# A fused transformer block on one core: row and context preparation one slot earlier, one low product of P at the slot's end, the first feed-forward rows in halves

## The reference, cut to what matters

```python
# x: (16, 256, 256) float32, cond_emb: (16, 256, 192); 16 heads of 64
def _attention(xq, xkv, wq, wk, wv, wo, bo):
    q, k, v = xq @ wq, xkv @ wk, xkv @ wv          # to 16 heads of 64
    attn = softmax(einsum('bihd,bjhd->bhij', q, k) * 64 ** -0.5)
    return einsum('bhij,bjhd->bihd', attn, v).reshape(B, S, 1024) @ wo + bo

h = _layernorm(x, ln1_g, ln1_b)
x = _attention(h, h, sa_wq, sa_wk, sa_wv, sa_wo, sa_bo) + x
h = _layernorm(x, ln2_g, ln2_b)
x = _attention(h, cond_emb, ca_wq, ca_wk, ca_wv, ca_wo, ca_bo) + x
h = _layernorm(x, ln3_g, ln3_b)
a, gate = split(h @ ff_w1 + ff_b1)                 # 256 -> 2 x 1024
return (a * gelu(gate)) @ ff_w2 + ff_b2 + x
```

## Time and profile before

| what | value |
|---|---|
| median of 3 runs | 1779.31 us (1778.8 to 1780.69) |
| profiled execution | 1778.15 us, span 1776.3 us |
| PE busy | 1736.4 us, 98% of the span |
| DVE busy | 1446.9 us, 81% |
| ACT busy | 1188.0 us, 67% |
| POOL busy | 1050.4 us, 59% |
| granted PE clock, mean | 0.999 |

### The profile page before, as it was taken

One profiled execution on the slowest core, in us unless ns is written; L12 is line 12 of the kernel. 1 busy time (PEld: TensorE's weight loads), 2 busy tenths in 40 slices (PEclk: granted clock), 3 DMA queues, 4 the chain that ended last, 5 costly groups with the idle time before them and its releaser, 6 DMA issues.

```text
span 1776.3 us, 43086 instructions
## 1 busy us (share of the span) xinstructions
PE 1736.4 (98%) x13824; PEld 1688.8 (95%) x13824; DVE 1446.9 (81%) x3137; ACT 1188.0 (67%) x3262; POOL 1050.4 (59%) x1791
## 2 busy tenths in 40 slices
PE   6999999999999999999999999999999998999998
PEld 5999999999999999999999999999999997888887
DVE  6888888888888888888888888888888887666664
ACT  5777777777777777777777777777777775221221
POOL 4777666666666666687777776666666654100110
PEclk9999999999999999999999999999999999999999
DMA  7766666666555555566676776666665561001000
GB/s 205 185 163 168 163 163 167 156 156 156 137 141 142 140 139 146 144 159 168 174 175 170 175 173 158 162 161 150 149 154 147 144 149 47 24 25 41 20 13 25
DMA packets 226496, 241.31 MB, mean 136 GB/s; under 512 B 68448, under 2 KB 190688, under 8 KB 226272
## 3 DMA queue, kind: packets, MB, share of 16 engines
q1 hardware_dynamic: 226272, 238.55, 54.0%
HBM read 58.08 MB, written 12.58 MB: 40 GB/s over the span
## 4 chain that ended last, share of the span: by engine, by line
PE 90%; POOL 5%; issue 3%; DVE 1%; ACT 0%; DMA 0%; SPq 0%; POOLq 0%; DVEq 0%; ACTq 0%
PE QKB L294 18%; PE PVB L354 13%; PE PTB L340 12%; PE WOP L327 9%; PE VB L313 9%; PE S L261 6%; PE S L262 6%; PE S L745 5%; PE PTB L745 5%; PE VB L758 3%; PE QKB L758 3%; PE VB L236 1%; POOL ON L647 1%; POOL VR L630 1%; POOL OT L652 1%
## 5 line engine op out<-in xcount | busy, mean ns | idle before, releaser
L410 ACT ACTIVATE PT<-S,NM 128x256 f32<-128x256 f32 x1024 | 471.7, 473 | 160.9 <-DVE NM L469 160.1
L469 DVE TENSOR_REDUCE NM<-S 128x2 f32<-128x512 f32 x512 | 329.6, 685 | 171.7 <-PE S L262 169.3
L647 POOL TENSOR_TENSOR ON<-ON,RB 128x256 f32<-128x256 f32 x256 | 188.6, 737 | 359.7 <-DVE ON L486 355.8
L429 ACT ACTIVATE PH<-PTB 128x1024 fp32r<-128x1024 f32 x256 | 263.2, 1028 | 126.0 <-PE PTB L340 125.8
L478 DVE TENSOR_TENSOR PL<-PTB,PH 128x512 fp32r<-128x512 f32 x512 | 327.3, 681 | 1.4 <-ACT PH L429 1.3
L340 PE MATMUL PTB<-IDN,PT 128*128 128x128 f32 x2048 | 265.9, 273 | 3.1 <-DVE PL L478 3.1
L261 PE MATMUL S<-RX 128*128 128x256 f32 x1024 | 256.9, 283 | 2.0 <-ACT PT L410 2.0
L262 PE MATMUL S<-RX 128*128 128x256 f32 x1024 | 256.7, 283 | 0.0
L340 PEld LDWEIGHTS PTB<-IDN,PT 128*128 128x128 f32 x2048 | 229.5, 140 | 4.5 <-ACT PT L410 3.8
L327 PE MATMUL WOP<-WO,OT 128*128 128x256 f32 x1536 | 226.5, 283 | 1.5 <-POOL OT L652 1.5
L294 PE MATMUL QKB<-HT,WA 128*128 128x256 f32 x1536 | 210.6, 287 | 6.6 <-POOL HT L552 3.6
(11 more groups left out here) (118 smaller groups left out, 3135.1 us busy)
## 6 DMA issues: line engine op xcount, KB each, us to landing
RX<-QKS SPq DMA_DIRECT2D x512, 192.0 KB, 2.9
RX<-QKS SPq DMA_DIRECT2D x512, 128.0 KB, 2.8
RB<-denominators SPq DMA_DIRECT2D x512, 64.0 KB, 2.6
out_dram<-XR SPq DMA_DIRECT2D x32, 256.0 KB, 3.0
XR<-in_x_dram SPq DMA_DIRECT2D x16, 256.0 KB, 3.1
denominators<-RDT SPq DMA_DIRECT2D x256, 16.0 KB
XR<-out_dram SPq DMA_DIRECT2D x16, 256.0 KB, 3.0
XN<-in_ctx_dram SPq DMA_DIRECT2D x16, 192.0 KB, 2.8
```

The costliest lines, as they stand in the source:

```text
L410: last = e.activation(PT[:, c % 2, j * S:(j + 1) * S], S1[:, i, qt * S:(qt + 1) * S], ACT.Exp, bias=NM[:, j:j + 1], accum_out=DEN[:, c % 2 ...
L429: e.activation(PH[:, s % 2, :], PTB[:, :, :].rearrange("p i n -> p (i n)"), ACT.Copy) \
L469: e.tensor_reduce(NM[:, i * TT:(i + 1) * TT], S1[:, i, :].rearrange("p (t s) -> p t s", t=TT), AX.X, ALU.max, negate=True).then_inc(a.dve_ ...
```

## The change

Four things are moved, and no arithmetic is added:

1. Preparation for the next sequence one slot earlier on every engine: statistics in slot 7 of the sequence before (was 0), aggregation and 1/sqrt in slot 0 (was 1), normalisation in slot 1 (was 2), context transposes in slots 0 and 1 (were 1 and 2), row transposes in slots 2 and 3 (were 3 and 4). SP loads the context in slot 5 (was 6).
2. On DVE the low product of head 0 of slot c-1 is done at the end of slot c, ahead of whatever closes the slot. The one of head 1 stays at the start of the next slot.
3. POOL splits staged weights in slots 4 to 7 (were 2 to 5; SP stages them in slot 1, was 0) and adds the bias to one tile in slot 5 and one in slot 6 (was two in slot 5).
4. The first feed-forward rows go in halves: statistics of two tiles each in ATT-9 and ATT-8, aggregation in ATT-7, normalisation of two tiles each in ATT-6 and ATT-5, four transposes each in ATT-3 and ATT-2, both through bank QKB, evacuated into the tile STG; the split by DVE at the end of ATT-1 (was ATT), as copy and subtraction of one half and then of the other.

```diff
 def pe_slot(e, sl):                       # TensorE, and the same shift in act_slot and pool_slot
-                if pair in (1, 2) and n >= B or pair in (3, 4):
+                if pair in (0, 1) and n >= B or pair in (2, 3):
                     sl.wait(e, a.dve_vf, c + 1)
-                if pair in (1, 2) and n >= B:
-                    pe_ctx(e, sl, n, pair - 1)
-                if pair in (3, 4):
-                    pe_h(e, sl, n, pair - 3)
+                if pair in (0, 1) and n >= B:
+                    pe_ctx(e, sl, n, pair)
+                if pair in (2, 3):
+                    pe_h(e, sl, n, pair - 2)
...
 def act_slot(e, sl):
-            if c == ATT - 1:
-                act_ffn_h(e, zero_ffn, 0)
+            if ATT - 3 <= c < ATT - 1:
+                act_ffn_h(e, zero_ffn, 0, c - ATT + 3)
...
+        def dve_p_low(e, s, i):
+
+            cols = slice(i * TT * S, (i + 1) * TT * S)
+            e.tensor_tensor(PL[:, cols], PTB[:, i, :], PH[:, s % 2, cols].bitcast(F32),
+                            ALU.subtract).then_inc(a.dve_pl, 1)
+
 def dve_slot(e, sl):
             if sl.has(c - 2):
-                s = c - 2
-                sl.wait(e, a.act_ph, s + 1)
-                sl.wait(e, a.pe_pv, s)
-                for i in range(2):
-                    cols = slice(i * TT * S, (i + 1) * TT * S)
-                    e.tensor_tensor(PL[:, cols], PTB[:, i, :], PH[:, s % 2, cols].bitcast(F32),
-                                    ALU.subtract).then_inc(a.dve_pl, 1)
+                dve_p_low(e, c - 2, 1)
...
+            if sl.has(c - 1):
+                sl.wait(e, a.act_ph, c)
+                sl.wait(e, a.pe_pv, c - 1)
+                dve_p_low(e, c - 1, 0)
+
             if pair == 3 and c > PAIRS:
...
+            if pair == PAIRS - 1 and c >= -1 and sl.has(PAIRS * (seq + 2)):
+                dve_await_x(e, sl, seq + 2)
+                dve_stats(e, sl, a, seq + 2)
             if prepares:
                 if pair == 0:
-                    dve_await_x(e, sl, seq + 1)
-                    dve_stats(e, sl, a, seq + 1)
+                    dve_aggregate(e, sl, a, seq + 1)
                 if pair == 1:
-                    dve_aggregate(e, sl, a, seq + 1)
-                if pair == 2:
                     if seq + 1 >= B:
                         e.wait_ge(a.pe_c, 2 * (seq + 2 - B))
                     dve_normalize(e, sl, a, seq + 1)
...
 def pool_weights(e, c):
-            if 2 <= pair < 2 + QTR and 1 <= seq <= NCH:
-                pool_split_w(e, WB, seq - 1, 2 + seq, pair - 2, 0)
+            if pair >= QTR and 1 <= seq <= NCH:
+                pool_split_w(e, WB, seq - 1, 2 + seq, pair - QTR, 0)
...
 def pool_slot(e, sl):
-            if prepares and pair == 5:
-                if seq + 1 == B:
+            if prepares and pair in (5, 6):
+                if seq + 1 == B and pair == 5:
                     e.wait_ge(d_bo, 32)
-                pool_add_bias(e, sl, a, seq + 1)
+                pool_add_bias(e, sl, a, seq + 1, pair - 5)
...
-            if prepares and pair == 1:
+            if prepares and pair == 0:
                 pool_rstd(e, sl, a, seq + 1)
...
+        def rows(chunk):
+
+            return (STG[:, 0:CW], STG[:, CW:2 * CW]) if chunk == 0 else halves(chunk)
+
         def transposes(chunk):
 
-            return (QKB, VB) if chunk == 0 else (PVB, WOP)
+            return (QKB, QKB) if chunk == 0 else (PVB, WOP)
...
 def pe_attention_slot(e, sl):
             pe_scores(e, sl)
-            if sl.c == ATT - 1:
+            if ATT - 3 <= sl.c < ATT - 1:
                 e.wait_ge(a.dve_lo, ATT)
-                e.wait_ge(a.dve_vf, ATT)
-                pe_ffn_h(e, zero_ffn, 0)
+                pe_ffn_h(e, zero_ffn, 0, sl.c - ATT + 3)
             pe_slot(e, sl)
...
 def dve_attention_slot(e, sl):
+            if c == ATT - 9:
+                e.wait_ge(a.dve_xo, B + HOLD + 2)
+                dve_stats(e, zero_ffn, fs, 0, 0, 1)
+            if c == ATT - 8:
+                dve_stats(e, zero_ffn, fs, 0, 2, 3)
             if c == ATT - 7:
-                e.wait_ge(a.dve_xo, B + HOLD + 2)
-                dve_stats(e, zero_ffn, fs, 0)
+                dve_aggregate(e, zero_ffn, fs, 0)
             if c == ATT - 6:
-                dve_aggregate(e, zero_ffn, fs, 0)
-            if c == ATT - 5:
                 e.wait_ge(a.pe_c, 2 * B)
                 e.wait_ge(a.pe_h, 4 * B)
                 e.wait_ge(a.pl_ht, 4 * B)
-                dve_normalize(e, zero_ffn, fs, 0, halves(0))
-            if c == ATT:
+                dve_normalize(e, zero_ffn, fs, 0, halves(0), (0, 1))
+            if c == ATT - 5:
+                dve_normalize(e, zero_ffn, fs, 0, halves(0), (2, 3))
+            if c == ATT - 1:
                 dve_ffn_split(e, zero_ffn, 0)
```

More of the change, by code:

```diff
@@ L302, in pe_slot @@
                 sl.wait(e, a.dve_vf, v)
-                if prepares and pair in (1, 2) and seq + 1 >= B:
-                    sl.wait(e, a.act_cf, 2 * (seq + 1 - B) + pair)
-                if prepares and pair in (3, 4):
-                    sl.wait(e, a.act_hf, 2 * (seq + 1) + pair - 2)
+                if prepares and pair in (0, 1) and seq + 1 >= B:
+                    sl.wait(e, a.act_cf, 2 * (seq + 1 - B) + pair + 1)
+                if prepares and pair in (2, 3):
+                    sl.wait(e, a.act_hf, 2 * (seq + 1) + pair - 1)
                 if v == 0:
@@ L397, in act_slot @@
             if c >= 0 and sl.has(PAIRS * (seq + 1)):
[L398 to L401 removed]
+                if pair in (0, 1) and seq + 1 >= B:
+                    act_ctx(e, sl, seq + 1, pair)
+                if pair in (2, 3):
+                    act_gain_bias(e, sl, seq + 1, pair - 2)
             if sl.has(c):
@@ L430, in act_slot, with dve_stats @@
                     .then_inc(a.act_ph, 1)
-        def dve_stats(e, sl, a, n):
-            for t in range(TT * sl.per):
+        def dve_stats(e, sl, a, n, *tiles):
+            for t in tiles or range(TT * sl.per):
                 last = e.bn_stats(ST6[:, t, :], XR[:, sl.x_cols(n, t * D, D)])
-            last.then_inc(a.dve_st, 1)
+                if t == TT * sl.per - 1:
+                    last.then_inc(a.dve_st, 1)
         def dve_aggregate(e, sl, a, n):
@@ L442, in dve_aggregate, with dve_normalize @@
             last.then_inc(a.dve_mv, 1)
-        def dve_normalize(e, sl, a, n, dest=(XN,)):
+        def dve_normalize(e, sl, a, n, dest=(XN,), tiles=()):
             sl.wait(e, a.pl_rs, n + 1)
-            for t in range(TT * sl.per):
+            for t in tiles or range(TT * sl.per):
                 last = e.tensor_scalar(dest[t // TT][:, t % TT * D:(t % TT + 1) * D], XR[:, sl.x_cols(n, t * D, D)],
                                        MV[:, t, 0:1], RSTD[:, t:t + 1], ALU.subtract, ALU.mult)
-            last.then_inc(a.dve_xn, 1)
+                if t == TT * sl.per - 1:
+                    last.then_inc(a.dve_xn, 1)
         def dve_await_x(e, sl, n):
@@ L533, in pool_rstd, with pool_add_bias @@
             e.tensor_tensor(RSTD[:, 0:tiles], VE[:, 0:tiles], MHALF[:, 0:tiles], ALU.pow).then_inc(a.pl_rs, 1)
-        def pool_add_bias(e, sl, a, n):
+        def pool_add_bias(e, sl, a, n, *tiles):
             sl.wait(e, a.dve_xn, n + 1)
-            for t in range(TT * sl.per):
+            for t in tiles or range(TT * sl.per):
                 xt = XR[:, sl.x_cols(n, t * D, D)]
                 last = e.tensor_tensor(xt, xt, BOUT[:, :], ALU.add)
-            last.then_inc(a.pl_xb, 1)
+                if t == TT * sl.per - 1:
+                    last.then_inc(a.pl_xb, 1)
         def pool_split_h(e, sl, n, k):
@@ L716, in w2, with pe_ffn_h @@
             return WA[:, 4 + f // 4, part, (f % 4) * D:(f % 4 + 1) * D]
-        def pe_ffn_h(e, sl, chunk):
+        def pe_ffn_h(e, sl, chunk, *ks):
             sl.wait(e, fs.dve_xn, chunk + 1)
-            sl.wait(e, fs.act_hf, PAIRS * chunk)
-            for k in range(KD):
+            for k in ks or range(KD):
+                sl.wait(e, fs.act_hf, KD * chunk + (k if ks else 0))
                 for t in range(2 * TT):
@@ L767, in pe_ffn, with act_ffn_h @@
                 pe_ffn_h(e, sl, chunk + 1)
-        def act_ffn_h(e, sl, chunk):
-            sl.wait(e, fs.pe_ht, PAIRS * (chunk + 1))
-            for k in range(KD):
-                last = e.activation(halves(chunk)[k], transposes(chunk)[k][:, :], ACT.Identity,
-                                    bias=LNG[:, 2, 1, k:k + 1], scale=LNG[:, 2, 0, k:k + 1])
-            last.then_inc(fs.act_hf, PAIRS)
+        def act_ffn_h(e, sl, chunk, *ks):
+            for k in ks or range(KD):
+                sl.wait(e, fs.pe_ht, KD * chunk + k + 1 if ks else KD * (chunk + 1))
+                e.activation(rows(chunk)[k], transposes(chunk)[k][:, :], ACT.Identity,
+                             bias=LNG[:, 2, 1, k:k + 1], scale=LNG[:, 2, 0, k:k + 1]).then_inc(fs.act_hf, 1)
         def act_ffn(e, sl):
@@ L1040, in weights @@
```

(6 more changed lines are left out.)

46 lines of the change are left out of this document (20 added, 26 removed).

## The result

The changed kernel takes 1789.01 us (median of 5 runs, 1787.53 to 1791.39), the kernel before 1779.31 us (median of 5 runs beside it, 1776.54 to 1781.19). The ratio is 1.0058 with a 95% interval of 1.0043 to 1.0072: slower by 9.7 us. The forecast was 1784, with a range of 1774 to 1793; 1789 is inside it, and 1 us above the 1781 to 1788 that the forecast claimed for itself.

The account below looks back on a forecast made before the run. PE, busy 98% of the span, was taken as the bound, its idle time mostly before the row transposes. Terms +17.1, -7.0, -1.0 and -3.5 sum to +5.6 us, giving 1784 us; 8-in-10 range 1774 to 1793.

Parts of the forecast that it names:

- The wait of the row transposes: PE's row transposes, slot 2: XN behind the moved product makes them wait 1.05 us in 30 places; term +17.1 us.
- The extra wait of the first sequence: Slot 2 of the first sequence: row transposes wait 1.9 us for PH, the product and XN; included in the +17.1.
- ON's loop: Plain cross-attention slots: one P-low product leaves the loop through ON to P·V, 0.11 us less in 64 slots, -7.0 us.
- the 0.11 is no wait: Rival, cross attention: the distance from P transposes to P·V belongs to the matmuls, nothing gained, 1791 us; chance 0.12.
- GpSimd: Weight splits and bias addition moved to other slots: two of PE's three waits for OT go, -1.0 us.
- The end: Last attention slots and first feed-forward rows: shorter loop, split normalisation, earlier split into RX, together -3.5 us, bounds -1 and -5.
- XN runs free of GpSimd: Rival: GpSimd's subtractions miss XN's start everywhere, transposes wait 0.81 us, growth +9.9, 1777.7 us; chance 0.26.
- XN is held twice: Rival: XN is held by subtraction, then cast or next subtraction; 1.38 us in 30 places, 1795 us; chance 0.12.
- The wait does not grow: Rival: the moved product costs XN nothing, the 16.3 us of waits stay, 1768 us; chance 0.08.

Follow-up runs that it names:

- e1: The changed kernel with VectorE's normalisation XN in slot 1 issued ahead of the moved P-low product instead of behind it: 1753.5 us.
- e3: The changed kernel with both P-low products back at the slot's start, leaving the shift, GpSimd's part and the new end: 1780.1 us.
- e4: The changed kernel with GpSimd's split of V in slot 2 waiting until XN is written: 1778.0 us.
- e2: The kernel before with only the first head's P-low product moved to the slot's end; preparation and program end untouched: 1797.3 us.
- e5: The kernel of e1 with the end of the program put back as in the kernel before: 1756.9 us.

## Why the prediction was right

*The wait of the row transposes* (+17.1, bounds +9.9 and +27.0). Mechanism and place were right: XN starts at +0.92 (+0.94 forecast), the transposes stand at +2.08 (+2.05), the slot of self attention waits 1.13 (1.09). e1, e3 and e4 show the cause from three sides. The size was low. The forecast took 1.05 for every wait; the fifteen of self attention sum to 17.1 (1.4 more than that), the fifteen of cross attention to 19.0 (3.2 more). By the slots a wait of cross attention is 1.28 in the mean, nine times 1.54 and six times 0.89. By the waits the term is 37.8 - 16.3 = +21.5. In cross attention the mechanism was only half right. The forecast let the subtraction for OT cover XN's start; it does overlap it, but in e4_pool_waits it does so as well and XN takes 0.73. What holds XN is V's CAST and the subtraction behind it. The long kind lies outside the bound of 1.38, which came from a pair of 1.30; the pair reaches 1.45.

One reading of the earlier trace rows was wrong. The prediction has XN's second instruction run beside GpSimd's CAST with no delay, and counts that against a full block. The instruction by itself, from the kernel before:

```profile
224.37 0.48 DVE L447 TENSOR_SCALAR XN<-XR,MV,RSTD 128x256 f32<-128x256 f32 x1
```

It takes 0.08 more than an undisturbed one (0.40) and ends at 224.85, 0.15 behind the CAST (224.70), as the first ends 0.15 behind the subtraction. XN was held twice there already; a CAST costs little because it is short.

*The extra wait of the first sequence* (1.9). The transposes stand at +2.78 there after a wait of 1.75, and the sequence as a whole costs the same 46.3 as before. The wait lies in the place of one of 1.60 that stood a slot later; both are inside the 37.8 and the 16.3.

*ON's loop* (-7.0). Right: 5.42 for 5.54 in four slots of each cross sequence, 60 x 0.12 = 7.2. e2 has it without the shift and e3 loses it without the move, so it is the product in the loop and nothing else. The rival "the 0.11 is no wait" falls.

*GpSimd* (-1.0). The two waits for OT went: slot 6 of sequences 1 and 2 fell from 6.27 to 5.66, 1.22 us together. That XN is held in these sequences now, since the splits have left, was not foreseen; it is inside the first term.

*The end* (-3.5). 2.30 + 1.04 = 3.3 by the stretches. Of this 1.1 comes with the move of P low alone (e2_p_low_alone against before) and 2.3 with the new end (e1 against e5). Slot ATT-4, with the wait of the earlier trace rows, fell from 7.21 to 6.31, the 0.9 of the forecast. ATT-3 takes 4.93, as forecast, but ATT-2 takes 5.22, and in ATT-1 and behind it P low of the second head stands behind other work, as PE's rows of the kernel after show.

```profile
1496.23 0.66 PE L340 MATMUL PTB<-IDN,PT 128*128 128x128 f32 x4 [0.68 <-DVE PL L465]
1499.08 0.98 PE L327 MATMUL WOP<-WO,OT 128*128 128x256 f32 x6 [0.85 <-POOL OT L660]
1501.81 0.65 PE L340 MATMUL PTB<-IDN,PT 128*128 128x128 f32 x4 [1.31 <-DVE PL L465]
```

The last wait is the one that the forecast halved the gain for, the split into RX standing ahead of that product. That the gains add up to the forecast of -3.5 is partly luck.

*The sum.* +21.5 - 7.2 - 1.2 - 3.3 = +9.8; the profiles differ by 10.8, of which 1.36 is the start of the program, so 9.4. Forecast +5.6. The difference is the mis-sized wait of the transposes, for the most part in cross attention; the other three terms are off by 0.2 each.

*The rivals.* "XN runs free of GpSimd" was priced at 0.81 per wait and 1777.7 us; e4 makes it true by force and measures 0.81 and 0.79, and 1778.0 us. "XN is held twice" (1.38, 1795) is not a rival but happens in part of the sequences of cross attention, in nine or fourteen of fifteen by the run, by the CAST first and the next subtraction second. "The wait does not grow" fails, since PH ends after VectorE is free: 0.68 us of idle time stand before the product. What the prediction did not consider is the kernel that the sum points to: the same change with two instructions exchanged.

## What to carry to other kernels

A piece of work that is moved into an engine's idle time brings its own wait along, and that wait holds all that is queued behind it: the product fitted VectorE's idle time, and the normalisation behind it paid. When work is moved, look for what another engine needs soonest and issue it ahead of anything that has to wait; here that order alone was worth 35 us, far more than any part of the change. A wait that a profile labels "issue" and that has no named releaser is found by comparing the position of the producer's end with the consumer's start in one slot of each kind.
